# Head rows of a decoder layer's scores: spread by SBUF-to-SBUF transfers in place of selection matmuls

## The reference

```python
x = tgt + _mha(tgt, tgt, tgt, sa_..., tgt_mask)       # self attention, masked
x = _layernorm(x, g1, be1)
x = x + _mha(x, memory, memory, ca_..., None)         # cross attention, 77 keys
x = _layernorm(x, g2, be2)
x = x + (relu(x @ w1 + b1) @ w2 + b2)
x = _layernorm(x, g3, be3)
# then, with query = x and key = value = memory
Q_phi, K_phi = elu(query), elu(key)
KV = einsum('bnd,bne->bde', K_phi, value)
Z = 1.0 / (einsum('bnd,bd->bn', Q_phi, K_phi.sum(axis=1)) + 1e-6)
x = query + einsum('bnd,bde->bne', Q_phi, KV) * Z[..., None]
# and a last layernorm with gamma, beta
```

## Time and profile before

| | |
|---|---|
| runs (3) | 343.69 us median, 342.73 to 345.12 |
| profiled execution | 342.77 us, of which 340.7 us span |
| TensorE busy | 289.0 us (85%), 3056 matmuls |
| VectorE busy | 261.5 us (77%), 867 instructions |
| ScalarE busy | 174.5 us (51%), 386 |
| GpSimd busy | 76.0 us (22%), 136 |
| DMA | 6.85 MB, 20 GB/s mean |

### The profile page before, as it was taken

One profiled execution on the slowest core, in us unless ns is written; L12 is line 12 of the kernel. 1 busy time (PEld: TensorE's weight loads), 2 busy tenths in 40 slices (PEclk: granted clock), 3 DMA queues, 4 the chain that ended last, 5 costly groups with the idle time before them and its releaser, 6 DMA issues.

```text
span 340.7 us, 8979 instructions
## 1 busy us (share of the span) xinstructions
PE 289.0 (85%) x3056; PEld 197.5 (58%) x3056; DVE 261.5 (77%) x867; ACT 174.5 (51%) x386; POOL 76.0 (22%) x136
## 2 busy tenths in 40 slices
PE   3769789989999999989998999899988986788551
PEld 2534555766775667656665676567755754565331
DVE  7664787878698979898898979897989784765524
ACT  2215445756565566646664656465754655336220
POOL 0410200211132112212231214112222224202421
PEclk9979999999999999999999999999999999589695
DMA  7500000000000000100000000000000000000000
GB/s 223 187 0 3 17 9 3 27 3 9 2 27 3 12 0 17 29 9 0 15 25 9 0 15 25 0 9 0 25 1 11 2 26 2 0 15 11 2 15 15
DMA packets 7506, 6.85 MB, mean 20 GB/s; under 512 B 744, under 2 KB 6712, under 8 KB 7480
## 3 DMA queue, kind: packets, MB, share of 16 engines
q1 hardware_dynamic: 7048, 6.38, 6.3%
q10 hardware_dynamic: 432, 0.14, 0.2%
HBM read 5.46 MB, written 1.05 MB: 19 GB/s over the span
## 4 chain that ended last, share of the span: by engine, by line
PE 54%; DVE 24%; issue 10%; ACT 5%; POOL 3%; DVEq 1%; DMA 1%; ACTq 0%; POOLq 0%; SPq 0%
PE proj_ps L399 10%; PE av_ps L370 7%; DVE neg_max L714 5%; PE s_ps L357 5%; PE s_ps L353 5%; PE s_ps L335 4%; PE proj_ps L465 3%; PE s_ps L332 3%; PE proj_ps L405 3%; POOL rstd L942 3%; PE s_ps L351 3%; PE proj_ps L467 2%; PE post_ps L389 2%; PE proj_ps L424 2%; PE post_ps L385 2%
## 5 line engine op out<-in xcount | busy, mean ns | idle before, releaser
L564 ACT ACTIVATE probs<-s_ps 128x512 f32<-128x512 f32 (+1 forms) x128 | 76.2, 595 | 57.4 <-PE s_ps L357 56.1
L714 DVE TENSOR_REDUCE neg_max<-s_ps 128x4 f32<-128x512 f32 (+1 forms) x128 | 71.6, 576 | 9.5 <-PE s_ps L335 9.2
L942 POOL TENSOR_TENSOR rstd<-var_e,neg_half 128x1 f32<-128x1 f32 x32 | 17.5, 547 | 181.8 <-DVE var_e L763 181.8
L357 PE MATMUL s_ps<-max_x,unit_sel 128*128 128x512 bf16 (+1 forms) x128 | 49.0, 383 | 3.6 <-DVE max_x L728 3.4
L399 PE MATMUL proj_ps<-x_t,w_sb 128*128 128x256 f32 x80 | 26.6, 455 | 1.0 <-issue 0.6
L335 PEld LDWEIGHTS s_ps<-sk_rows,sq_wide 128*128 128x128 bf16 x256 | 20.6, 101 | 10.3 <-issue 1.6
L570 ACT COPY av_sb<-av_ps 128x256 f32<-128x256 f32 x32 | 11.9, 372 | 27.3 <-PE av_ps L370 27.3
L335 PE MATMUL s_ps<-sk_rows,sq_wide 128*128 128x128 bf16 x256 | 25.7, 225 | 0.0
L332 PE MATMUL s_ps<-bias_q,id_b 128*128 128x512 bf16 x64 | 25.4, 397 | 0.0
L353 PE MATMUL s_ps<-cq_wide,ck_rows 128*77 128x512 bf16 x64 | 24.8, 387 | 0.0
L351 PE MATMUL s_ps<-bias_k,id_b 128*128 128x512 bf16 x64 | 24.7, 386 | 0.0
(11 more groups left out here) (131 smaller groups left out, 657.7 us busy)
## 6 DMA issues: line engine op xcount, KB each, us to landing
xt_in<-in_x_t SPq DMA_DIRECT2D x8, 128.0 KB, 2.0
out<-o_all SPq DMA_DIRECT2D x8, 128.0 KB, 1.8
row_sb<-in_rows SPq DMA_DIRECT2D x1, 832.0 KB, 6.5
w_sb<-in_weights SPq DMA_DIRECT2D x1, 768.0 KB, 10.4
ct_in<-in_ctx_t SPq DMA_DIRECT2D x8, 77.0 KB, 1.8
cn_in<-in_ctx_n SPq DMA_DIRECT2D x8, 77.0 KB
w_sb<-in_weights SPq DMA_DIRECT2D x2, 128.0 KB, 2.8
id_f<-in_ident ACTq DMA_DIRECT2D x1, 64.0 KB, 2.6
```

What stands on the lines that cost most here:

```text
L357: nc.tensor.matmul(bank[0:n, :], unit_sel[:, u, 0:n], max_x[:, b, :, :], start=False, stop=True).then_inc(M["s2_ready"], 1)
L564: nc.scalar.activation(probs[0:n, u, :], s2_ps[u % 2][0:n, :], ACT.Exp, scale=SCALE).then_inc(M["exp_done"], 1)
L714: nc.vector.tensor_reduce(neg_max[:, b, RH * u:RH * (u + 1)], scores, AX_X, ALU.max, negate=True).then_inc(M["max_done"], 1)
L942: nc.gpsimd.tensor_tensor(rstd[:, b, :], var_e[:, b, :], neg_half[:, 0:1], ALU.pow).then_inc(M["rstd_ready"], 1)
```

## The change

- The selection matmuls, the spread matrices and ScalarE's casts are gone. SP issues, for each kind and group (both batches together), eight SBUF-to-SBUF transfers: four for q, four for k. Each takes hi or lo as it is (128 partitions x 256 columns, 154 for cross keys) and lands on every fourth of 32 partitions, four units side by side. The columns of the q and k weights and biases are permuted on the host so that the rows fall in place.
- `widen` stays on VectorE. It takes both batches at once: four copies of 1024 columns per kind and group, of cross attention two at (0, 2) and two at (0, 3), of self attention two at (2, 1) and two at (2, 2). `query_major` waits at unit 0 for all four (`RH * (g + 1)`) and for the k transfers.
- `rows_k` and `wide` have two buffers by group; `rows_q` has one. SP waits for the lo part, for the copies of the group before (q) and for the key-major scores of two groups before (k). ScalarE's `split_hi` waits for the transfers of the group before.
- `xt_in` and `ct_in` have two buffers and two semaphores each; x of group 1 and context of group 0 are loaded at the start, the others an iteration earlier.
- The hardware loop is gone: all twelve iterations are written out.

```diff
@@ order of the uses of the two banks
-        ("yc0", TAIL, 0, 0), ("cv", CROSS, 0, 0), ("cq0", CROSS, 0, 1), ("ck0", CROSS, 0, 2), ("sqk", NEXT, 0, 3),
-        ("yc1", TAIL, 1, 0), ("cq1", CROSS, 1, 0), ("ck1", CROSS, 1, 1), ("h01", TAIL, 1, 1), ("h23", TAIL, 1, 2),
-        ("ff", TAIL, 1, 4),
-        ("ys0", SELF, 2, 0), ("sq0", NEXT, 2, 0), ("sk0", NEXT, 2, 1), ("kv", TAIL, 2, 2), ("sv", NEXT, 2, 3),
-        ("yt", TAIL, 2, 4),
-        ("ys1", SELF, 3, 0), ("sq1", NEXT, 3, 0), ("sk1", NEXT, 3, 1), ("cqk", SELF, 3, 2), ("la", TAIL, 3, 3)]
+        ("yc0", TAIL, 0, 0), ("cv", CROSS, 0, 0), ("sqk", NEXT, 0, 3),
+        ("yc1", TAIL, 1, 0), ("h01", TAIL, 1, 1), ("h23", TAIL, 1, 2), ("ff", TAIL, 1, 4),
+        ("ys0", SELF, 2, 0), ("kv", TAIL, 2, 2), ("sv", NEXT, 2, 3), ("yt", TAIL, 2, 4),
+        ("ys1", SELF, 3, 0), ("cqk", SELF, 3, 2), ("la", TAIL, 3, 3)]
...
@@ SP
+            def spread_rows(i, name):
+                kind = name[0]
+                g = i - (NEXT if kind == "s" else SELF)
+                wait_read(sp, i, name)
+                wait_reuse(sp, M["wide_" + kind], RH * g)
+                for s in range(4):
+                    sp.dma_start(rows_q[kind][s:P:4, :, :, :].rearrange("p u b n -> p u (b n)"),
+                                 part_of(kind + "q", s)[:].rearrange("p b n -> p (b n)")).then_inc(
+                        M[f"spread_{kind}q"], 16)
+                s2_done(sp, kind, g - 2)
+                for s in range(4):
+                    sp.dma_start(rows_k[kind][s:P:4, g % 2, :, :, :].rearrange("p u b n -> p u (b n)"),
+                                 part_of(kind + "k", s)[:].rearrange("p b n -> p (b n)")).then_inc(
+                        M[f"spread_{kind}k"], 16)
...
             sp.dma_start(w_sb[:, 4:N_W, :], weights[:, 4:N_W, :]).then_inc(M["w_rest"], 16)
+            load_ct(0)
+            load_xt(1)
...
-                if on(i, SELF):
+                if i > NEXT and on(i + 1, SELF):
                     if on(i, CROSS):
                         wait_full(sp, i, "cv")
                     settle()
...
+                    load_ct(i + 1)
+                if on(i, NEXT):
+                    spread_rows(i, "sqk")
                 if on(i, LAST):
...
+                if on(i, SELF):
+                    spread_rows(i, "cqk")
...
@@ TensorE, query_major
                 if u == 0:
-                    pe.wait_ge(M[f"wide_{kind}"], G * g + b + 1)
-                    wait_rows(pe, kind, "k", b, g)
+                    pe.wait_ge(M["wide_" + kind], RH * (g + 1))
+                    wait_spread(pe, kind + "k", g)
...
@@ ScalarE, split_hi
+                g = i - (NEXT if kind == "s" else SELF)
+                if g > 0:
+                    wait_spread(act, kind + "q", g - 1)
+                    wait_spread(act, kind + "k", g - 1)
...
@@ VectorE
+            def widen(kind, g, heads):
+                wait_spread(dve, kind + "q", g)
+                s2_done(dve, kind, g - 2)
+                for j in heads:
+                    nc.vector.tensor_scalar(wide[kind][:, g % 2, j, :, :, :], rows_q[kind][:], row_is_j[:, j:j + 1],
+                                            None, ALU.mult).then_inc(M["wide_" + kind], 1)
...
                 for name in uses_at(i, k, u):
                     if name in ("sqk", "cqk"):
                         split_lo(i, name, name[0])
+                if k == 0 and u in (2, 3) and on(i, CROSS):
+                    widen("c", i - CROSS, range(2 * u - 4, 2 * u - 2))
+                if k == 2 and u in (1, 2) and on(i, NEXT):
+                    widen("s", i - NEXT, range(2 * u - 2, 2 * u))
```

More of the change, by code:

```diff
@@ L118, in wait_reuse, with run_iterations @@
             eng.wait_ge(sem, value)
-    def run_iterations(eng, iteration):
-        for i in range(NEXT, TAIL + 1):
-            iteration(i)
-        with eng.Fori(TAIL + 1, NG - 1) as i:
-            iteration(i)
-        for i in range(NG - 1, NG + LAST):
+    def run_iterations(iteration):
+        for i in range(NEXT, NG + LAST):
             iteration(i)
@@ L144, in decoder_layer_kernel @@
         id_b = sb("id_b", [P, P], BF16)
-        spread = {(side, part): sb(f"spread_{side}_{part}", [P, UNITS, 4, 32], BF16)
-                  for side in "qk" for part in ("hi", "lo")}
         row_is_j = sb("row_is_j", [P, RH])
@@ L334, in query_major @@
                 for j in range(RH):
-                    last = nc.tensor.matmul(bank[:, j * n:(j + 1) * n], wide[kind][:, b, j, u, :],
-                                            rows_qk[kind + "k"][:, b, u, :], start=(kind == "c"), stop=True,
+                    last = nc.tensor.matmul(bank[:, j * n:(j + 1) * n], wide[kind][:, g % 2, j, u, b, :],
+                                            rows_k[kind][:, g % 2, u, b, :], start=(kind == "c"), stop=True,
                                             skip_group_check=True)
@@ L455, in linear_attention @@
                 last.then_inc(full("la"), 1)
-            def spread_rows(i, name):
-                kind, side, b = name[0], name[1], int(name[2])
-                n = KLEN[kind] if side == "k" else S
-                wait_read(pe, i if kind == "s" else i - 1, kind + "qk")
-                bank = open_bank(i, name)
-                for u in range(UNITS):
-                    nc.tensor.matmul(bank[:, u * n:(u + 1) * n], spread[side, "hi"][:, u, :, :],
-                                     hi[kind + side][:, b, :], start=True, stop=False)
-                    last = nc.tensor.matmul(bank[:, u * n:(u + 1) * n], spread[side, "lo"][:, u, :, :],
-                                            lo[kind + side][:, b, :], start=False, stop=True)
-                last.then_inc(full(name), 1)
             def light_work(i, k, u):
@@ L686, in _ @@
             dve.wait_ge(M["id_set"], 1)
-            for (side, part), tile in spread.items():
-                for s in range(4):
-                    if (s // 2 if side == "q" else s % 2) == (part == "lo"):
-                        last = nc.vector.tensor_copy(tile[:, :, s, :], id_b[:].rearrange("p (u m) -> p u m", u=UNITS))
-            last.then_inc(M["spread_set"], 1)
-            by_row = id_f[:].rearrange("p (s j i) -> p j s i", s=4, j=RH)
             by_head = id_f[:, 0:2 * NH].rearrange("p (c u j) -> p c u j", c=2, u=UNITS)
-            nc.vector.tensor_reduce(row_is_j[:], by_row, AX_XY, ALU.add)
+            by_row = id_f[:].rearrange("p (j r) -> p j r", j=RH)
+            nc.vector.tensor_reduce(row_is_j[:], by_row, AX_X, ALU.add)
             nc.vector.tensor_reduce(max_is_j[:], by_head.rearrange("p c u j -> p j c u"), AX_XY, ALU.add)
@@ L783, in split_lo @@
                 last.then_inc(read(name), 1)
-            def widen(i, name):
-                key, b = name[:2], int(name[2])
-                wait_read(dve, i, name)
-                for j in range(RH):
-                    last = nc.vector.tensor_scalar(wide[name[0]][:, b, j, :, :], rows_qk[key][:, b, :, :],
-                                                   row_is_j[:, j:j + 1], None, ALU.mult)
-                last.then_inc(M["wide_" + name[0]], 1)
+            def widen(kind, g, heads):
[4 more added lines that the diff above has]
+                                            None, ALU.mult).then_inc(M["wide_" + kind], 1)
             def store_v(i, name, kind, bias):
@@ L987 @@
     sk = c.shape[1]
+    hd = d // NH
+    rows_first = np.arange(d).reshape(UNITS, RH, hd).transpose(1, 2, 0).reshape(d)
+    for n in ("sa_qw", "sa_kw", "ca_qw", "ca_kw", "sa_qb", "sa_kb", "ca_qb", "ca_kb"):
+        a[n] = a[n][..., rows_first]
     square = ["sa_qw", "sa_kw", "sa_vw", "sa_ow", "ca_qw", "ca_kw", "ca_vw", "ca_ow"]
```

88 lines of the change are left out of this document (36 added, 52 removed).

## The result

The changed kernel takes 359.80 us (median of 4 runs, 357.87 to 360.72) against 344.02 us (4 runs, 342.73 to 345.12): ratio 1.0453, 95% interval 1.040 to 1.051. The profiled execution took 360.72 us, its span is 358.7 us, 18.0 more than before. The direction was forecast, the size was not: I had said 351 and at most 357.5.

The account below looks back on a forecast made before the run. It took VectorE as tight as TensorE in k=0, and TensorE as tight in k=1. Start +3.5, iteration 0 -1.2, iteration 1 -0.4, iterations 2 to 6 +5.3, iteration 7 +0.8 gave +8.0: 351 us, range 340 to 357.5.

Parts of the forecast that it names:

- The mechanism: At k=1's first cross scores: TensorE idles 3.0 us for all four copies, e_k 2 us later; chance 0.54.
- the sum: Whole kernel: start and iterations 0, 1, 2 to 6, 7 add to +8.0 us, giving 351 us.
- the forecast gain of 1.2 us: Iteration 0: four self groups go, no cross wait, VectorE's batch 1 copies leave the chain: -1.2 us.
- The start: First transfers queue behind SP's loads; first key-major product 4.4 us later, 0.9 back from the clock: +3.5, bounds 2 and 5.5.
- Iterations 1 and 6 to 8: Iteration 1 -0.4 us; iteration 6 as a full one, +1.05; iteration 7 +0.8 for the cross wait; iteration 8 0.
- The hardware loop: Writing out all iterations is neither better nor worse: 0, bounds 0.4 us per iteration both ways.
- No change: Rival, chance 0.23: same wait, but TensorE's saved 3.2 us pay through slack in the e_k chain; 346, from 341 to 347.
- Faster, TensorE sets the iteration: Rival, chance 0.15: VectorE's copies at (0,3) are done when TensorE asks; 2.4 us less in each of five iterations, about 331.
- Late transfers: Rival, chance 0.08: landings don't overlap, each takes 2 us; scores 4 to 5 us late in seven iterations, about 370.
- the exclusion of the two: Copies at (0,3) would wait for GpSimd's residual add: some 0.25 us per iteration, 1.5 in all, left to the upper end.

## Why the prediction was wrong in size

**The mechanism was right, point by point.** TensorE idles in front of the first cross scores, 2.63 us for a forecast 3.0. A pair of 1024-column copies takes 0.87 us (0.8). lo ends 2.87 us behind sqk's mark (3.0 by the forecast, with the mark 0.7 us earlier than 152.90), e_k comes 2.4 us later against sqk (2), and no transfer is late after the start. TensorE's busy time falls by 17 us rather than 25, since part of it is now done at the lower clock: with the cross copies at (0, 2) and a mean clock of 0.956 the same matmuls took 267.8 us, with the first transfers ahead of the weights and 0.921 they took 276.3 (the trace after, at 271.7, lacks 22 of their records). In iteration 2, written out in both kernels and at full clock, the price is 0.89 us against 1.05; moving the copies one unit ahead takes all of it back, and more.

**The step that failed is the sum.** It has four mis-sized terms.

- *The clock behind the new idle time*: no term at all. I forecast that TensorE would stand idle for 3 us in every iteration, and used the granted clock only at the start, where the earlier trace rows shows 0.70 behind an idle stretch. That row was the warning. With TensorE kept busy the same kernel takes 6.8 us less. In iteration 0 there is no such wait, but the selection matmuls that had filled its gaps are gone; the clock stands at 0.50 for six microseconds, and the forecast gain of 1.2 us is +0.1. That this removal is what lowered the clock there is argued from the windows; no run put the work back. In the kernel with copies batch by batch and the first transfers from ScalarE, the clock in the same two windows was 0.64 and 1.00, and iteration 0 took 22.80 us, which is the forecast's -1.2.
- *The start*: +5.1 us, forecast +3.5 within 2 to 5.5. The copies ended at 19.4 as worked out (19.5), and the first key-major product came at 26.4, not 25.2; the 0.9 us expected back from the clock did not come, since TensorE still ran at the lower level at 26.41 (0.63 us for 512 columns). With the transfers from ScalarE's queue it did come: copies done at 19.56, full clock by 24.76, first key-major product at 25.63, and the mark 3.2 us later than before, close to the forecast. So what this term missed is the clock again, and in that it was not the same in every execution.
- *Iterations 1 and 6 to 8*: with TensorE kept busy through the wait they still lose 0.6 and 3.2 us, forecast -0.4 and +1.85. I had cost them as a full iteration less some parts, not followed them.
- *The hardware loop*: 0, with 0.4 us per iteration as a bound both ways; it is 0.35 in the change's favour. I had read 0 off a looped and an unlooped iteration with different work on VectorE. So the looped iterations lost 0.5 us at full clock, for a forecast of 1.05.

Without the falls of the clock that the unread matmuls removed, the change would have cost 18.0 - 6.6 = 11.4 us of the span, where I had 8.0. So they made 6.6 of the 10 us missed: 351 and 6.6 are 357.6, the upper end of the range, and the start, the first iterations and the tail took the time past it. The slow clock of the start and of iteration 0 is not in the 6.6 us, so the clock's part is larger than that.

**The rivals.** *No change* rested on slack in the e_k chain; there is none at full clock (iteration 2 lost 0.89 us) and less than none otherwise. *Faster, TensorE sets the iteration*: wrong for this kernel, yet its price was about right for the other order, where iterations 3 to 5 fell by 1.4 us with all cross copies at (0, 2) and by 2.4 batch by batch, 0.35 of it the loop's. *Late transfers*: an issue on SP takes 0.60 to 0.65 us where I took 0.45, but landings overlap and the eight were in time. They were late once, at the start: SP issued the first at 10.41 us, behind the loads, and the q transfers took 3.6 to 3.7 us to land.

**GpSimd and VectorE.** I had left the exclusion of the two to the upper end of the range. At the start it is decisive, and there it hides: the earlier trace rows showed it (3.28 us for four copies beside the addition), and I used that row for the length of the copies without asking what would come of it with rows that arrive earlier. The Trainium skill, "SBUF — State Buffer", section "Who interferes with whom", says that a copy, a cast or a tensor_scalar of VectorE in its fast mode and a GpSimd instruction exclude each other for a whole instruction; the traces agree, with 4.06 us for a cast of 16 columns beside an addition of 4.49 us. In the iterations it cost next to nothing: the pair of copies at (0, 3) took 0.87 us, the pair at (0, 2) 0.88, since GpSimd's residual addition (165.10 to 165.56) was over when the pair began at 165.51.

**What stays open.** Why the clock fell in every other iteration of the profiled execution, with the same idle time of 2.63 us in each, and in other iterations of kernels that differ only at the start; and what made it fall in iteration 1 of one of two nearly equal kernels. A fall can also cost more than the 1.3 us here: with GpSimd's addition behind the copies, iteration 3 took 39.00 us at a mean clock of 0.91, iterations 4 and 5 took 37.76 and 37.77 at 0.95.

## What to carry to other kernels

When an engine's queue gets a new wait, price the place of the awaited instruction before its amount: two copies one unit earlier were worth 19.6 us (the falls of the clock that they end are part of it), and twice as many instructions, batch by batch, were faster than half of them at once. When a change takes filler work from TensorE or gives it an idle time of some microseconds, add what the slower clock costs behind it; a run with unread matmuls in the gap tells the wait's own price from the clock's. And when two causes cover one stretch (a late transfer and a held engine), removing either alone shows little, so try them together before calling either innocent.

## What the runs showed of the hardware

- TensorE's granted clock fell from 2.4 to 1.2 GHz behind idle times of 2.63 us, in some iterations and not in others; in iterations 1, 3 and 5 of the kernel after a fall cost 1.26 to 1.35 us (512 columns in 0.63 us rather than 0.38, for 2 to 3 us). At the start the same work, from the first scores to the mark of iteration 0, took 10.0 or 12.2 us, by when the clock rose.
- A GpSimd tensor_tensor of 128x2048 float32 (4.5 us) held VectorE's copies and casts in SBUF to its end (5.70 us for four copies that take 1.67; 4.06 for a cast that takes 0.17). Maxima that read PSUM kept their 0.69 us beside it.
- An SBUF-to-SBUF transfer of 64 KB onto every fourth partition takes SP 0.60 us to issue and lands 1.9 us later. Beside the first loads it took 3.6 to 3.7 us from SP's queue, and 4.4 to 5.9 from ScalarE's, issued 2.5 us earlier.
- A masked copy of 1024 bf16 columns takes 0.40 us from one to the next (four in 1.67 us), of 512 columns 0.28 (four in 1.14), so twice the columns cost 1.4 times as much.
- A hardware loop cost 0.35 us per iteration against the same code written out.
